# A two-layer expert kernel on one core: the moving operands placed off the weights' 512-byte grid

## What is computed

```python
g = jnp.einsum('bsd,edf->ebsf', h, Wg)             # e: 8 experts, f: 512
u = jnp.einsum('bsd,edf->ebsf', h, Wu)
expert_outs = jnp.einsum('ebsf,efd->ebsd', jax.nn.silu(g) * u, Wd)
expert_output = jnp.einsum('be,ebsd->bsd', gating_probs, expert_outs)
shared = jnp.einsum('bsf,fd->bsd', jax.nn.silu(h @ Sg) * (h @ Su), Sd)
x = x + (1.0 - sg) * expert_output + sg * shared
x = x + jnp.einsum('bij,bjk->bik', T[itok - 1], x)
```

## Time and profile before

| | us |
|---|---|
| time, median of 2 runs | 312.02 |
| lowest, highest | 311.98, 312.07 |
| profiled execution, its time | 312.09 |
| profiled execution, its span | 310.1 |

### The profile page before, as it was taken

One profiled execution on the slowest core, in us unless ns is written; L12 is line 12 of the kernel. 1 busy time (PEld: TensorE's weight loads), 2 busy tenths in 40 slices (PEclk: granted clock), 3 DMA queues, 4 the chain that ended last, 5 costly groups with the idle time before them and its releaser, 6 DMA issues.

```text
span 310.1 us, 4762 instructions
## 1 busy us (share of the span) xinstructions
PE 305.5 (99%) x1364; PEld 253.3 (82%) x1364; DVE 217.5 (70%) x355; ACT 164.6 (53%) x306; POOL 102.2 (33%) x116
## 2 busy tenths in 40 slices
PE   8999999999999999999999999999999999999996
PEld 7688888888888888888888888888888888888885
DVE  2786667766676666776667766677666766668885
ACT  5565555555555555555555555555555555555552
POOL 2565312441155115511552134411441155111310
PEclk9999999999999999999999999999999999999999
DMA  6930300030001100030003001100013000000112
GB/s 159 201 89 2 103 1 2 0 94 7 1 0 45 56 0 0 0 101 0 0 0 109 13 13 17 17 14 13 15 17 110 0 0 0 0 2 0 34 36 68
DMA packets 32727, 10.39 MB, mean 34 GB/s; under 512 B 16208, under 2 KB 32720, under 8 KB 32720
## 3 DMA queue, kind: packets, MB, share of 16 engines
q1 hardware_dynamic: 32720, 10.30, 13.5%
HBM read 9.25 MB, written 1.05 MB: 33 GB/s over the span
## 4 chain that ended last, share of the span: by engine, by line
PE 95%; SPq 1%; DMA 1%; POOL 0%; DVE 0%; ACT 0%; issue 0%
PE o_bank L470 11%; PE o_bank L473 11%; PE o_bank L471 11%; PE g_bank L446 10%; PE u_bank L446 10%; PE g_bank L445 10%; PE u_bank L445 10%; PE g_bank L444 10%; PE u_bank L444 10%; DMA w_raw<-in_L_cond_Wd 1%; PE o_bank L491 1%; SPq L158 1%; PE o_bank L483 0%; POOL w_lo L212 0%; DVE res L371 0%; PE u_bank L483 0%
## 5 line engine op out<-in xcount | busy, mean ns | idle before, releaser
L342 DVE TENSOR_TENSOR u_bank<-u_bank,silu_g 128x512 f32<-128x512 f32 x144 | 100.7, 699 | 84.2 <-PE u_bank L446 82.6
L278 ACT ACTIVATE silu_g<-g_bank 128x512 f32<-128x512 f32 x144 | 86.1, 598 | 132.8 <-PE g_bank L446 132.4
L348 DVE TENSOR_TENSOR h_lo<-u_bank,h_hi 128x512 fp32r<-128x512 f32 x144 | 97.9, 680 | 0.1
L260 POOL TENSOR_TENSOR acc<-acc,scaled 128x512 f32<-128x512 f32 x32 | 41.5, 1296 | 163.2 <-DVE scaled L356 163.0
L284 ACT ACTIVATE h_hi<-u_bank 128x512 fp32r<-128x512 f32 x144 | 85.4, 593 | 0.7 <-DVE u_bank L342 0.7
L470 PE MATMUL o_bank<-h_hi,w_hi 128*128 128x512 f32 x144 | 56.2, 390 | 0.8 <-POOL w_lo L212 0.8
L444 PE MATMUL u_bank<-x_hi,w_hi 128*128 128x512 f32 x144 | 56.1, 390 | 0.0
L473 PE MATMUL o_bank<-h_lo,w_hi 128*128 128x512 f32 x144 | 56.0, 389 | 0.0
L445 PE MATMUL u_bank<-x_lo,w_hi 128*128 128x512 f32 x144 | 56.0, 389 | 0.0
L471 PE MATMUL o_bank<-h_hi,w_lo 128*128 128x512 f32 x144 | 56.0, 389 | 0.0
L446 PE MATMUL u_bank<-x_hi,w_lo 128*128 128x512 f32 x144 | 56.0, 389 | 0.0
(11 more groups left out here) (49 smaller groups left out, 151.2 us busy)
## 6 DMA issues: line engine op xcount, KB each, us to landing
w_raw<-in_L_cond_Wd SPq DMA_DIRECT2D x8, 256.0 KB, 3.9
w_raw<-in_L_cond_Wg SPq DMA_DIRECT2D x7, 256.0 KB, 3.1
w_raw<-in_L_cond_Wu SPq DMA_DIRECT2D x7, 256.0 KB, 3.8
T_blk<-in_L_cond_T SPq DMA_DIRECT2D x64, 16.0 KB, 1.6
out_y<-res SPq DMA_DIRECT2D x3, 256.0 KB, 2.3
x_blk<-in_x SPq DMA_DIRECT2D x4, 128.0 KB, 3.6
x_nat<-in_x SPq DMA_DIRECT2D x1, 256.0 KB, 2.8
x_blk<-in_x SPq DMA_DIRECT2D x4, 64.0 KB, 2.7
```

Of the source, the lines that this page charges most:

```text
L260: nc.gpsimd.tensor_tensor(acc[:, t, :], acc[:, t, :], scaled[:, t % 2, :], ALU.add).then_inc(acc_done, 1)
L278: nc.scalar.activation(silu_g[:, k % 2, :], g_bank[k % 2][:, :], ACT.Silu).then_inc(g_read, 1)
L342: nc.vector.tensor_tensor(u_bank[k % HR][:, :], u_bank[k % HR][:, :], silu_g[:, k % 2, :], ALU.mult).then_inc(h_done, 1)
L348: nc.vector.tensor_tensor(h_lo[:, k % HR, :], u_bank[k % HR][:, :], h_hi[:, k % HR, :].bitcast(F32), ALU.subtract).then_inc(split_done, 1)
```

## The change

The rows of `x_hi`, `x_lo`, `h_hi` and `h_lo` become ROW = 640 elements long instead of 512, and the 512 elements in use start inside each row at an offset that is another one for each x tile and each h slot. Two small functions, `X(a, t)` and `H(a, slot)`, give the slice, and each instruction that reads or writes these four tensors uses them.

```diff
+    ROW = W + P
+    X_AT = [16, 32, 64, 96]
+    H_AT = [48, 80, 112, 8]
...
-        x_hi = sb("x_hi", [P, NT, W], F32R)
-        x_lo = sb("x_lo", [P, NT, W], F32R)
+        x_hi = sb("x_hi", [P, NT, ROW], F32R)
+        x_lo = sb("x_lo", [P, NT, ROW], F32R)
...
-        h_hi = sb("h_hi", [P, HR, W], F32R)
-        h_lo = sb("h_lo", [P, HR, W], F32R)
+        h_hi = sb("h_hi", [P, HR, ROW], F32R)
+        h_lo = sb("h_lo", [P, HR, ROW], F32R)
...
+        def X(a, t):
+            return a[:, t, X_AT[t]:X_AT[t] + W]
+
+        def H(a, slot):
+            return a[:, slot, H_AT[slot]:H_AT[slot] + W]
...
-                nc.scalar.activation(h_hi[:, k % HR, :], u_bank[k % HR][:, :], ACT.Copy).then_inc(h_rounded, 1)
+                nc.scalar.activation(H(h_hi, k % HR), u_bank[k % HR][:, :], ACT.Copy).then_inc(h_rounded, 1)
...
-                nc.vector.tensor_tensor(h_lo[:, k % HR, :], u_bank[k % HR][:, :], h_hi[:, k % HR, :].bitcast(F32),
+                nc.vector.tensor_tensor(H(h_lo, k % HR), u_bank[k % HR][:, :], H(h_hi, k % HR).bitcast(F32),
...
-                product(g_bank[k % 2][:, :], (k // U % 2, c, 0), x_hi[:, t, :], x_lo[:, t, :],
+                product(g_bank[k % 2][:, :], (k // U % 2, c, 0), X(x_hi, t), X(x_lo, t),
```

More of the change, by code:

```diff
@@ L232, in split_x @@
                 pool.wait_ge(x_rounded, t + 1)
-                nc.gpsimd.tensor_tensor(x_lo[:, t, :], acc[:, t, :], x_hi[:, t, :].bitcast(F32),
+                nc.gpsimd.tensor_tensor(X(x_lo, t), acc[:, t, :], X(x_hi, t).bitcast(F32),
                                         ALU.subtract).then_inc(acc_done, 1)
@@ L293, in round_x @@
                 act.wait_ge(x_turned, t)
-                nc.scalar.activation(x_hi[:, t, :], acc[:, t, :], ACT.Copy).then_inc(x_rounded, 1)
+                nc.scalar.activation(X(x_hi, t), acc[:, t, :], ACT.Copy).then_inc(x_rounded, 1)
             def round_w0(c, m):
@@ L306, in _ @@
             act.wait_ge(x0_turned, 1)
-            nc.scalar.activation(x_hi[:, 0, :], o_bank[0][:, :], ACT.Copy).then_inc(x_rounded, 1)
+            nc.scalar.activation(X(x_hi, 0), o_bank[0][:, :], ACT.Copy).then_inc(x_rounded, 1)
             act.wait_ge(w0_in, 32)
@@ L384, in _ @@
             dve.wait_ge(x_rounded, 1)
-            nc.vector.tensor_tensor(x_lo[:, 0, :], o_bank[0][:, :], x_hi[:, 0, :].bitcast(F32),
+            nc.vector.tensor_tensor(X(x_lo, 0), o_bank[0][:, :], X(x_hi, 0).bitcast(F32),
                                     ALU.subtract).then_inc(split_done, 1)
@@ L460, in project_u @@
                     pe.wait_ge(split_done, EARLY + n + 1 - HR)
-                product(u_bank[k % HR][:, :], (k // U % 2, c, 1), x_hi[:, t, :], x_lo[:, t, :],
+                product(u_bank[k % HR][:, :], (k // U % 2, c, 1), X(x_hi, t), X(x_lo, t),
                         True, True).then_inc(u_done, 1)
@@ L469, in project_down @@
                 pe.wait_ge(h_rounded, n + 1)
-                nc.tensor.matmul(o_bank[t % 2][:, :], w_hi[:, w[0], w[1], w[2], :], h_hi[:, slot, :], start=c == 0, stop=False)
-                nc.tensor.matmul(o_bank[t % 2][:, :], w_lo[:, w[0], w[1], w[2], :], h_hi[:, slot, :], start=False, stop=False)
+                nc.tensor.matmul(o_bank[t % 2][:, :], w_hi[:, w[0], w[1], w[2], :], H(h_hi, slot), start=c == 0, stop=False)
+                nc.tensor.matmul(o_bank[t % 2][:, :], w_lo[:, w[0], w[1], w[2], :], H(h_hi, slot), start=False, stop=False)
                 pe.wait_ge(split_done, EARLY + n + 1)
-                last = nc.tensor.matmul(o_bank[t % 2][:, :], w_hi[:, w[0], w[1], w[2], :], h_lo[:, slot, :],
+                last = nc.tensor.matmul(o_bank[t % 2][:, :], w_hi[:, w[0], w[1], w[2], :], H(h_lo, slot),
                                         start=False, stop=c == NC - 1)
@@ L509, in _ @@
             pe.wait_ge(x_rounded, 1)
-            nc.tensor.matmul(g_bank[0][:, :], w_hi[:, 0, 0, 0, :], x_hi[:, 0, :], start=True, stop=False)
+            nc.tensor.matmul(g_bank[0][:, :], w_hi[:, 0, 0, 0, :], X(x_hi, 0), start=True, stop=False)
             pe.wait_ge(split_done, 1)
-            nc.tensor.matmul(g_bank[0][:, :], w_lo[:, 0, 0, 0, :], x_hi[:, 0, :], start=False, stop=False)
+            nc.tensor.matmul(g_bank[0][:, :], w_lo[:, 0, 0, 0, :], X(x_hi, 0), start=False, stop=False)
             pe.wait_ge(split_done, EARLY)
-            nc.tensor.matmul(g_bank[0][:, :], w_hi[:, 0, 0, 0, :], x_lo[:, 0, :], start=False, stop=True).then_inc(g_done, 1)
+            nc.tensor.matmul(g_bank[0][:, :], w_hi[:, 0, 0, 0, :], X(x_lo, 0), start=False, stop=True).then_inc(g_done, 1)
             project_u(0, 0)
             pe.wait_ge(w_ready, 1)
-            product(g_bank[1][:, :], (0, 1, 0), x_hi[:, 0, :], x_lo[:, 0, :], True, True).then_inc(g_done, 1)
+            product(g_bank[1][:, :], (0, 1, 0), X(x_hi, 0), X(x_lo, 0), True, True).then_inc(g_done, 1)
             project_u(1, 1)
```

## The result

The changed kernel takes 317.64 us (2 runs, 317.60 to 317.69) against 312.02 us: ratio 1.019, 95% interval 1.0172 to 1.0208. It is slower by 5.6 us, 1.9%, where no change was forecast. The time lies inside the stated range (305.0 to 319.0), but the forecast, no change, was wrong: the interval lies clear of 1. Whether the rise reaches 2% it leaves open.

The account below looks back on a forecast made before the run. The prediction took TensorE's matmul count times pitch as the bound. It put every term at 0: 312.09 + 0 = 312.1 us for an execution like the profiled one, so 312.0 us predicted, range 305.0 to 319.0.

Parts of the forecast that it names:

- What bounds the kernel: TensorE, busy 99% of the span and waiting for nobody: number of matmuls times pitch, 1296 x 0.2267 = 293.8 of 310.1 us.
- The pitch doesn't vary with distance so far: All 118 matmuls of a group last 389 ns at distances to the weights from 4 KB to over 50 KB.
- Another start distance only changes the order in which the two meet the same places, not how often: TensorE's weight load and moving read shift 1186 bytes during one load, so each matmul keeps 226.7 ns: 0 us.
- The rule of the Trainium skill: TensorE has two independent read ports, so loading the next weights takes no bandwidth and distance is worth nothing: 312.0 us.
- The third reading: Slower pitch at equal addresses after transposes; a new distance might pick it: 232 ns, 6.9 us more, 318.9 us; slower 0.15.
- a small slowdown of 1 to 2%: The slower half of a small effect of some offsets, 1 to 2% in either direction, 0.10 evenly split.
- the single 0.24 us: Each matmul goes at the slowest step seen after the transposes: 1296 x 13 ns = 17 us more, 329 us.
- Nothing is added or removed: The same instructions stand in the same order, so the sum of counts is unchanged.
- The faster rival: A start elsewhere removes a clash of TensorE's two reads: 11.5 us less, 300.5 us, or 306 if half help; chance 0.13.
- the 13.4 ns over 213.3: Excess of the matmul pitch over 512 columns at 2.4 GHz, all the change could win: 17.4 us, floor 294.6 us.
- the estimate beside it: The skill's pitch of columns / 2.4 + 2.5 ns, 215.8 ns for TensorE's matmuls here: 14.1 us less, 297.9 us.
- What would show it: Signs in g's first matmul: right, 2.040 us units; faster, below 2.00 us; slower, medians above 389 ns or a spread.

Follow-up runs that it names:

- the map: Five runs of the changed kernel with x and h offsets by tile, four also with odd experts' weights moved: 318.33, 318.64, 320.64, 318.79 and 319.21 us.

## Why the prediction was wrong, step by step

**What bounds the kernel** was right: pitch times 1296, with the other engines covered. TensorE's own work is 99% of the chain, VectorE and ScalarE kept 681 and 593 ns off the grid, and the change could act only through the pitch.

**"The pitch doesn't vary with distance so far"** was a right reading with too small a reach, as it said itself (the 4 KB to 50 KB are those of all nine matmuls of a unit; the group shown has 22 to 39 KB). All distances seen were multiples of 512, where the pattern repeats every 256: they were one and the same case, looked at 118 times. Their number said nothing about the rest.

**"Another start distance only changes the order in which the two meet the same places, not how often"** is the step that failed. The price for it is in the map: 2.040 to 2.130 us a unit by the start distance alone, and 2.060 us whether x and h or the weights are moved (2.083 us in the changed kernel). The step took two mean speeds, the load's from its duration and the matmul's from its pitch, and reasoned on how often the reads meet, without a row that tied the number of meetings to a time. Even its own count didn't hold: 1186 bytes are 2.3 rounds of 512, no whole number, so that how often a place is met would depend on the start. The term that it put at nothing was 1296 x 4.8 ns = 6.2 us. The runs show that a travelling weight read makes the start distance count and that a matmul's pitch depends on those before it, as the turn of 229 and 237 ns at one distance does. How the store serves two reads, and why 0 and 256 are best, stays open; no run here shows it.

**The rule of the Trainium skill**, "TensorE: Matmul & The Clock Gate", section "Step-by-step: what each phase is for", that loading the next weights takes no bandwidth from the running matmul, would have given 312.0 us. The measurement decides: moving only the weights' block made the unit 20 ns longer, so the two reads are not independent in this kernel.

**The third reading**, that slower states of the pitch exist at equal addresses and that a new distance might pick one, was the right one. I gave it 0.15, and a small slowdown of 1 to 2%, which is what was measured, 0.05, because it rested on few matmuls and because they faded. Its size came out: 232 ns and 318.9 us, against 231.5 ns and 317.6 us measured. That is luck in part: single distances have from 228.9 to 236.7 ns, and the mean of the eight offsets chosen happens to lie where the five matmuls of the earlier trace rows do. Its dearer form, "the single 0.24 us", was a misreading of starts shown to 10 ns: in nanoseconds that step is 234, and the five are 235, 234, 235, 225 and 231. The slow steps fade within a few matmuls where the distance is 0 or 256; where it isn't, they stay.

**"Nothing is added or removed"** held. **The faster rival** fell: no distance tried had a pitch below 226.7 ns on average, so the 13.4 ns over 213.3 aren't a clash that one of these offsets removes. Nor did any come near the 215.8 ns of the estimate beside it. What the 13.4 ns are stays open; no run leaves out a load.

**What would show it** named the right sign, medians above 389 ns and a spread at some offsets.

## What to carry to other kernels

A measurement that has seen only one value of what the change varies, however many times, bounds nothing: the zero effect here should have had both ends of the range and no more. Where float32r matmuls run back to back with a new weight load each, place the weights and the moving operands at a distance that is a multiple of 256 bytes from each other, and look at such a pad or an odd tile size when the pitch is some nanoseconds long; a few operands off the grid slow the others too. A transient in the trace of before, such as the slow matmuls after a burst, shows what the hardware can do, and here gave a fair price for the case that the change makes it permanent.

## What was not expected of the hardware

The pitch is exact: in the steady stretch every unit at a distance of 0 takes 2.040 us, and with contiguous weights each deviation repeats within 1 ns from expert to expert, so that 1 ns in 227 can be read from one profile where the time of a run can't show it.

The time of a run has a part that isn't: TensorE's wait for the first down projection's `w_lo`, at the start, was 0.8 us in the profile of before, nothing in the changed kernel's, 0.7 us with all at 64 bytes and 0.2 to 1.1 us in the others; in some a g product at 7 to 8 us also waited for its `w_lo`, 0.8 us in the longest case (all moved together). The ten runs of the kernel with rows alone lie between 311.34 and 312.95 us. A difference under 1 us between single runs of this kernel says nothing about its steady stretch.

Eight bytes of distance cost more (2.104 us) than 64 (2.060 us); the price doesn't follow the size of the offset in either direction.
